# Row loads on ScalarE's queue, ranks in bf16 and norms behind the third round, in a fused Mamba, experts and attention kernel

## What is computed

```
Mamba:      norm, projection, convolution, a scan over 1024 positions with 16 states for each of
            256 channels, output projection, residual (the token stream is called X below)
experts:    p = softmax(norm(X) @ gate_W); the two best of 8 experts of each token;
            y = x + relu(x @ W1[e] + b1[e]) @ W2[e] + b2[e], mixed; norm, gain, add to X, norm
attention:  6 layers, 16 heads of 8, every token against all 1024 of its batch, softmax,
            a decay by distance, feed-forward 128-512-128, norms
last:       feed-forward with weights and activations rounded to 4-bit blocks of 16, residual
```

## Time and profile before

| | |
|---|---|
| median of 3 executions | 2826.67 us (2818.91 to 2829.14) |
| the profiled execution | 2813.64 us, its span 2811.8 us |
| busy in the span | DVE 2458.1 us (87%), PE 2392.2 (85%), ACT 2302.9 (82%), POOL 1433.5 (51%) |
| granted TensorE clock, mean | 0.94 of full speed |

### The profile page before, as it was taken

One profiled execution on the slowest core, in us unless ns is written; L12 is line 12 of the kernel. 1 busy time (PEld: TensorE's weight loads), 2 busy tenths in 40 slices (PEclk: granted clock), 3 DMA queues, 4 the chain that ended last, 5 costly groups with the idle time before them and its releaser, 6 DMA issues.

```text
span 2811.8 us, 93918 instructions
## 1 busy us (share of the span) xinstructions
PE 2392.2 (85%) x38335; PEld 1274.7 (45%) x38335; DVE 2458.1 (87%) x3438; ACT 2302.9 (82%) x4212; POOL 1433.5 (51%) x2865
## 2 busy tenths in 40 slices
PE   6778684788998998999889989899999998999856
PEld 3444473434444444444444444445444444444435
DVE  4988943699999999999999899999999999999956
ACT  5877632579998998999999899999999999999832
POOL 3443454235644665456644566445664456643564
PEclk8988887689999999999999999999999999999978
DMA  4000023413122131221222121221212212120000
GB/s 134 1 1 1 23 77 87 82 32 61 23 44 47 31 53 30 47 41 36 44 39 47 34 44 31 52 47 32 45 31 52 47 33 45 31 36 11 2 1 16
DMA packets 75119, 110.44 MB, mean 39 GB/s; under 512 B 7425, under 2 KB 69761, under 8 KB 72129
## 3 DMA queue, kind: packets, MB, share of 16 engines
q1 hardware_dynamic: 72256, 99.35, 18.5%
q0 software_dynamic: 2432, 5.08, 0.6%
HBM read 79.41 MB, written 29.05 MB: 39 GB/s over the span
## 4 chain that ended last, share of the span: by engine, by line
PE 38%; issue 18%; ACT 11%; DVE 11%; POOL 9%; DMA 1%; DVEq 0%; SPq 0%; ACTq 0%; POOLq 0%
PE bank L767 12%; PE bank L698 12%; PE bank L778 10%; ACT E L1038 9%; DVE NM L1409 7%; ACT acc L989 1%; POOL acc L1626 1%; POOL H L1636 1%; PE bank L679 1%; POOL H L1639 1%; POOL smp L1619 1%; DMA UNITB<-second 1%; PE bank L692 1%; POOL dg L1684 1%; ACT UB L1000 1%
## 5 line engine op out<-in xcount | busy, mean ns | idle before, releaser
L1409 DVE TENSOR_REDUCE NM<-bank 128x1 f32<-128x1024 f32 x1536 | 1800.2, 1208 | 82.4 <-PE bank L767 62.3
L1038 ACT ACTIVATE E<-bank,NM 128x1024 f32<-128x1024 f32 x1536 | 1707.5, 1118 | 189.0 <-DVE NM L1409 139.5
L767 PE MATMUL bank<-KS,QS 72*32 72x512 bf16 x12288 | 975.1, 390 | 163.5 <-ACT E L1038 113.7
L778 PE MATMUL bank<-E,dg 128*32 128x256 f32 x12288 | 941.2, 387 | 6.0 <-issue 4.2
L1684 POOL TENSOR_TENSOR dg<-mask,RZ 128x128 f32<-128x128 f32 x384 | 153.0, 398 | 863.7 <-DVE RZ L1419 758.4
L767 PEld LDWEIGHTS bank<-KS,QS 72*32 72x32 bf16 x12288 | 260.9, 96 | 706.3 <-ACT E L1038 583.2
L778 PEld LDWEIGHTS bank<-E,dg 128*32 128x32 f32 x12288 | 393.6, 112 | 297.0 <-issue 71.3
L1038 ACT ACTIVATION_READ_ACCUMULATOR E<-bank,NM 128x1 f32 x1536 | 310.6, 202 | 0.0
L1626 POOL TENSOR_TENSOR acc<-acc,rel 128x256 f32<-128x256 f32 x384 | 272.3, 729 | 7.8 <-ACT acc L989 7.8
L698 PE MATMUL bank<-H,ET 128*32 128x129 f32 x6144 | 194.9, 277 | 13.7 <-issue 7.3
L698 PEld LDWEIGHTS bank<-H,ET 128*32 128x32 f32 x6144 | 175.4, 111 | 41.5 <-issue 18.7
(11 more groups left out here) (262 smaller groups left out, 2651.7 us busy)
## 6 DMA issues: line engine op xcount, KB each, us to landing
KS<-scratch SPq DMA_DIRECT2D x72, 384.0 KB
QS<-scratch SPq DMA_DIRECT2D x216, 128.0 KB
scratch<-UB SPq DMA_DIRECT2D x144, 128.0 KB
WL<-in_wl SPq DMA_DIRECT2D x6, 1091.0 KB, 12.1
first<-in_fill SPq DMA_DIRECT2D x2, 990.0 KB, 8.2
second<-in_fill SPq DMA_DIRECT2D x2, 990.0 KB, 10.2
WAX<-first SPq DMA_DIRECT2D x2, 528.0 KB, 4.8
UNITB<-second SPq DMA_DIRECT2D x2, 528.0 KB, 13.5
```

The source lines that it names most:

```text
L767: inst = PE_.matmul(bank[x % 3][32 * i:32 * i + 32, k * 512:k * 512 + 512], QS[0:72, half % 2, 4 * hq + i, r0:r0 + 32], KS[0:72, b, 4 * hq ...
L778: inst = PE_.matmul(pb(6)[32 * k:32 * k + 32, 256 * grp:256 * grp + 256], dg[:, x // 4 % 3, x % 4, :], E[:, x % NE, :].rearrange("p (i k c ...
L1038: A_.activation(E[:, x % NE, :], bank[x % 3][:, :], ACT.Exp, bias=NM[:, x % 4:x % 4 + 1], accum_out=ZS[:, quad % 3, j:j + 1]).then_inc(s[" ...
L1409: V.tensor_reduce(NM[:, x % 4:x % 4 + 1], bank[x % 3][:, :], AX.X, ALU.max, negate=True).then_inc(s["rowmax"], 1)
```

## The change

1. `rows_of` for rounds 1 to 3 is issued by ScalarE's program, just before the round's first unit, and no longer by SP.
2. The registers are loaded at other places (`KNOWN`): for rounds 0 and 1 VectorE does it in steps 120 and 126 of the scan, TensorE at 122 and 149; for rounds 2 and 3 one to three steps ahead of the round. VectorE copies a unit's `W1` one step earlier.
3. `rank` works on bf16 copies (`OH`, `below`, `ones`) with 9 products for 16.
4. The second batch's gating (`G00` to `G30`) and its rank stand at 143 to 150, inside round 0 and ahead of round 1 (`ROUND[1]` 151), where most of it stood inside round 1. For this the last output product and its norm move ahead (`LASTLY`: `outp` at 137 for 144).
5. Three norms of the first batches and tiles (`n00`, `n01`, `n02`) go from VectorE to GpSimd, and `beta` is added earlier.
6. The first batch's `f0` to `n21` stand at 179 to 186, from the last units of round 2 on; the projections follow at 186 to 196, and round 3 starts at step 190 (184 before), after the first half's projection.
7. `KS` is laid out `[2, 2, 16, 512]` for `[2, 16, 1024]`, so that what `stack_k` writes to a partition is one run of 16 KB for 16 runs of 1 KB.

```diff
-DONE = {"PE": {16: "outp"}, "ACT": {}, "DVE": {4: "y2", 17: "x1"}, "POOL": {5: "yz0", 6: "yz1"}}
+DONE = {"PE": {14: "outp"}, "ACT": {}, "DVE": {4: "y2", 14: "x1"}, "POOL": {5: "yz0", 6: "yz1"}}
+LASTLY = {"PE": {9: "outp"}, "ACT": {}, "DVE": {4: "y2", 10: "x1"}, "POOL": {5: "yz0", 6: "yz1"}}
...
-ROUND = (133, 150, 167, 184)
+ROUND = (133, 151, 168, 190)
+KNOWN = {"PE": {122: 0, 149: 1, 167: 2, 189: 3}, "DVE": {120: 0, 126: 1, 166: 2, 187: 3}}
...
-        KS = sbuf(pk, "KS", [128, 2, NHEAD, L], BF16)
+        KS = sbuf(pk, "KS", [128, 2, 2, NHEAD, 512], BF16)
...
-        OH = sbuf(pm, "OH", [128, NT, 16])
+        OH = sbuf(pm, "OH", [128, NT, 16], BF16)
+        below, ones = sbuf(pm, "below", [128, 128], BF16), sbuf(pm, "ones", [128, 128], BF16)
...
                 for r, u in rounds(p):
-                    if u == 0:
-                        chosen = experts_of(e, mybir.EngineType.PE, r)
-                    unit_pe(e, r, u, chosen)
+                    unit_pe(e, r, u, chosen[r])
+                if p in KNOWN["PE"]:
+                    chosen[KNOWN["PE"][p]] = experts_of(e, mybir.EngineType.PE, KNOWN["PE"][p])
...
-                PE_.matmul(o[:, 0:128], mc_("below"), OH[:, batch(j), :].rearrange("p t c -> p (t c)"), start=True, stop=False)
+                PE_.matmul(o[:, 0:128], below[:, :], OH[:, batch(j), :].rearrange("p t c -> p (t c)"), start=True, stop=False)
+                PE_.matmul(o[:, 128:144], ones[:, :], OH[:, 8 * j + 7, :], start=False, stop=False)
                 for t in range(7):
-                    PE_.matmul(o[:, 16 * t + 16:128], mc_("ones"), OH[:, 8 * j + t, :].unsqueeze(1).to_broadcast([128, 7 - t, 16]), start=False, stop=(t == 6))
-                for t in range(8):
-                    inst = PE_.matmul(o[:, 128:144], mc_("ones"), OH[:, 8 * j + t, :], start=(t == 0), stop=(t == 7))
+                    inst = PE_.matmul(o[:, 16 * t + 16:144], ones[:, :], OH[:, 8 * j + t, :].unsqueeze(1).to_broadcast([128, 8 - t, 16]), start=False, stop=(t == 6))
...
@@ scan_act
                 for r, u in rounds(p):
+                    if r and u == 0:
+                        rows_of(e, r)
                     unit_act(e, r, u)
...
@@ scan_dve
+                for r, u in rounds(p + 1):
+                    if u < UNITS:
+                        weights_dve(e, UNITS * r + u, chosen[r][u])
...
@@ sync
             e.wait_ge(s["dtp"], 2 * CHUNKS)
-            rows_of(0)
+            rows_of(e, 0)
...
-            rows_of(1)
-            rows_of(2)
             mixed_of(0)
             store_qk(e, 0)
             stack_k(e, 0)
             stack_q(e, 0)
-            rows_of(3)
             store_qk(e, 1)
             stack_k(e, 1)
             mixed_of(1)
```

More of the change, by code:

```diff
@@ L66, in side @@
     for k in range(CHUNKS):
-        out += [(k, x) for x in DONE[engine].get(p - 32 * (k + 1), "").split()]
+        done = DONE if k < CHUNKS - 1 else LASTLY
+        out += [(k, x) for x in done[engine].get(p - 32 * (k + 1), "").split()]
         if k:
@@ L767, in scores @@
                         inst = PE_.matmul(bank[x % 3][32 * i:32 * i + 32, k * 512:k * 512 + 512], QS[0:72, half % 2, 4 * hq + i, r0:r0 + 32],
[L768 removed]
+                                          KS[0:72, b, k, 4 * hq + i, :], start=True, stop=True)
                 inst.then_inc(s["scores"], 1)
@@ L1176, in scan_dve @@
                 for r, u in rounds(p):
-                    if u == 0:
-                        chosen = experts_of(e, mybir.EngineType.DVE, r)
-                    unit_dve(e, own, r, u, chosen)
+                    unit_dve(e, own, r, u)
                 for j, x in gates("DVE3", p):
@@ L1193, in expert_dve @@
                 e.wait_ge(s["ld_moe"], 128)
+                own.count(V.tensor_copy(below[:, :], mc_("below")))
+                own.count(V.tensor_copy(ones[:, :], mc_("ones")))
                 for q in range(2):
@@ L1556, in expert_pool @@
                 G.tensor_tensor(EN[k][3][:, r], EN[k][2][:, r], mhalf[:, 0:4], ALU.pow).then_inc(s["epow"], 1)
+            elif p == "n0":
+                e.wait_ge(s["epow"], NORM[0, j] + 1)
+                for i in range(4 * j, 4 * j + 4):
+                    G.tensor_scalar(row(i), X[:, i, :], EN[0][1][:, i, 0:1], EN[0][3][:, i:i + 1], ALU.subtract, ALU.mult).then_inc(s["rn"], 1)
             elif p == "bet":
```

48 lines of the change are left out of this document (25 added, 23 removed), and 27 rows, old and new, of tables (GATES, PROJECT).

## The result

The changed kernel took 2790.11 us (median of 4 executions, 2785.40 to 2801.01) beside 2823.08 us for the kernel before (4, 2818.91 to 2829.14): ratio 0.9883, 95% interval 0.9861 to 0.9906, or 33 us less. The forecast was 2808 us, 18.4 us less. The direction and the place were right; the size was not, and the time lies at the lower end of the range. Three later comparisons of the same two kernels gave 0.9893 (0.9858 to 0.9928), 0.9880 (0.9841 to 0.9919) and 0.9929 (0.9910 to 0.9948).

The account below looks back on a forecast made before the run. It took attention to be bound by VectorE and ScalarE together, the seam by successive waits. Terms -2.6 - 2 - 6 - 2 - 5.8 = -18.4 us, from a median of 2826.67, gave 2808 us; range 2790 to 2821.

Parts of the forecast that it names:

- the scan: Up to round 0: norms and a register load leave VectorE, two register loads come in; -2.6 us (-8 to +3).
- round 0: Gating, last output product and a norm come earlier, filling GpSimd's idle time before the last scatter; -2 us (-2 to +2).
- round 1: The rank no longer stands between the units but mostly under the round trip before them; -6 us (-6.9 to -3).
- round 2 to the first keys: VectorE's 8.55 us wait at f0 goes, but units and norms overlap less; -2 us (-5 to +5).
- first keys to first scores: Earlier rows for round 3 shorten the key chain by 9.8 us, the layout costs 4; -5.8 us (+2 to -14).
- 27.3 + 5: At the seam: queries through 27.3 us after the first KS issue, then 5 us for the second half's six stores.
- From `KS` issued to the first scores is 14.6 us and stays.: At the seam's end: issue of KS to first scores unchanged at 14.6 us, but for the layout.
- +2 each: Each of two KS loads in the seam's chain slower by 2 us through the new layout.
- The rest: Attention and last feed-forward, behind the first scores: no change, since keys come 33.8 us or more ahead of use.
- A shorter seam: Rival, chance 0.20: layout no slower, stores in 3 us, register loads 1.2 each, perhaps 2 from norms; about 2797 us.
- The queue doesn't matter: Rival, chance 0.10: round 3's rows share DMA engines with KS and QS and arrive no earlier; 2815 us.
- Slower: Rival, chance 0.05: attention's key loads grow slow enough to delay the scores; 2844 us at 37 us a load.

Follow-up runs that it names:

- e13: The kernel before, unedited, profiled again on a chip without late signals; median 2814.77 us on that chip, first scores at 529.15 us.
- e14: The changed kernel, unedited, on the same chip as e13; ratio 0.9880 to the kernel before, first scores at 498.17 us.
- e7: The kernel before, unedited, profiled again on a chip with late signals; first scores at 546.55 us.
- e8: The changed kernel, unedited, on the same chip as e7; ratio 0.9893 to the kernel before, first scores at 512.25 us.
- e15: The kernel before with only the row loads of rounds 1 to 3 issued by ScalarE; 2793.74 us beside 2814.77, ratio 0.9930.
- e1: The kernel before with only the new KS layout; 2826.57 us beside 2829.69, ratio 1.0001.
- e2: The changed kernel with the old KS layout back; 2796.89 us, ratio 0.9898 to the kernel before.
- e9: The changed kernel with the second batch's gating, rank (still bf16) and last output product back at their old steps; ratio 0.9874 to the kernel before.
- e4: The changed kernel with the register loads of rounds 0 and 1 moved back next to the rounds; ratio 0.9891 to the kernel before.
- e16: The changed kernel with the second half's stores and keys ahead of the first half's queries on SyncE; 2777.43 us, ratio 0.9850 to the kernel before.
- e12: The changed kernel with the second half's six stores issued by ScalarE's queue at step 197; ratio 0.9896 to the kernel before.
- e18: The changed kernel, unedited, on a further chip with late signals; ratio 0.9929 to the kernel before, first scores at 515.01 us.
- e3: The changed kernel with SyncE issuing the rows of rounds 1 to 3 again; 2819.40 us, ratio 0.9961 to the kernel before.
- e5: The changed kernel with the first batch's f0 to n21 moved from steps 179 to 186 to 171 to 179; ratio 0.9903 to the kernel before.

## Why the prediction was right, and where it was wrong

The terms, by the pair from one chip of kind A (e13, e14), which is the kind the trace of before was taken on, and by the pair on B (e7, e8):

| term | forecast (bounds) | A | B |
|---|---|---|---|
| the scan (to round 0's start) | -2.6 (-8 to +3) | +0.4 | -3.6 |
| round 0 | -2 (-2 to +2) | -4.1 | -0.9 |
| round 1 | -6 (-6.9 to -3) | -8.8 | -14.4 |
| round 2 to the first keys | -2 (-5 to +5) | +1.2 | +11.0 |
| first keys to first scores | -5.8 (+2 to -14) | -19.8 | -26.5 |
| sum | -18.4 | -31.0 | -34.3 |

**The step that failed is the last term**, first keys to first scores: -5.8 us forecast, -19.8 measured on A. Its mechanism was right: the long wait of the earlier trace rows is gone, the queries' transfers run through round 3, and the first scores wait for `KS`, not for GpSimd. The second half's stores still land behind the queries, as I had said. Its size came out of three sub-steps, each wrong by 4 to 5.5 us.

- *From the first keys to the second half's.* I had 27.3 + 5; in e14 it is 26.8, 5.5 less. The 27.3 was the landing of round 3's first rows, which I took for the end of the queries. By the trace's packets the queries ended 26.0 us after the first keys were asked for in the trace of before, and 27.2 in e13, with the rows of round 3 moving beside them; in e15, without those rows, it is 22.4, in e14 23.3. That is 4.0 us. The stores need 3.5 more for my 5: half of their packets (384 of 768) have moved by 474.8, among the queries, and the other half starts at 482.5, just ahead of the queries' end at 484.2. That is 1.5 us.
- *"From `KS` issued to the first scores is 14.6 us and stays."* Those 14.6 us ended with GpSimd's last scatter and the fence; the load itself takes 10.5 in e14, 4.1 less. I read two rows and not what lies between them, though the chain of the trace of before shows the scatters there, the last of them ending at 530.31.
- *"+2 each" for the layout.* The key loads of e1, e2 and e15 show none of it, 4 less.

Together 13.6 us, which is the difference between -5.8 and -19.8 but for 0.4.

**Round 1** was right in kind: the 6.85 us of the rank go and nothing sticks out. On A it gave 2.8 us more than forecast. The load and the rank are done in 3.25 + 0.50 us (e14) where I had 3.1 to 7.4, but they lie ahead of the round's first transpose and don't shorten the round; and the gating pieces are not it either, since e9 has them inside the round at the same 26.0 us. e9 shows that bf16 would have sufficed without the move. In e13 the step that holds the rank takes 8.9 us for 1.23, 7.7 too many; what gave the rest stays open. On B the round lost 52.0 - 34.8 = 17.2 us more before and 11.6 more in the changed kernel: which goes with the chip and the place in the program, and which no row of the trace of before could show.

**The scan** came out at nothing on A instead of -2.6. The two register loads were dearer in my sum (4.8) than the trace has them (one gap of 1.31 us that e4 removes). What the sum had at nothing is the wait behind GpSimd's scatters, 4.57 us in e14: they stand in the upper bound ("if GpSimd's eight scatters of the first batch hold the sums up anyway"), but I had priced only GpSimd's own 1.8 us and not what stands ahead of it in its queue.

**Round 0** gave 4.1 us on A, outside my -2 to +2, but one pair can't carry that: three kernels on A that are alike up to there have 31.8, 33.7 and 36.0 us (e14, e16, e12). The start of round 0 scatters as well, 355.29 to 356.59 in the same three.

**Round 2** gave nothing on A, as its bounds allowed. On B it cost 11 us, because there, in the kernel before, the longer round 1 had given GpSimd time to finish: `H` is asked for 1.1 us after round 2's first transpose (9.6 in e13), and `f0` did not wait at all. The 2.5 us for the rising clock were worked out from no row; in e14 the clock stood at 0.50 until 4.4 us into the round.

**The rest** was left at nothing. My sign of being wrong, more than 5 us longer, shows in e14 (2288.4) and e18 (2287.6) against 2281.0, and not in the other two; since variants of the changed kernel have 2270 to 2282, I read it as drift, which is not shown. In e18 the changed kernel measured only 0.9929, though its first scores came as early as in the other profiles from B. The kernel before was not profiled on that chip, so whether its seam is shorter there or the rest of the changed one longer stays open.

**The signs.** No float32 rank, no wait at `f0`, the queries running through round 3 and first scores that wait for `KS` all came as said. Of the two gaps at the register loads one came (1.31 us, step 126). That the first profile of the change had its first scores at 514.52, inside my 510 to 515, was luck: on the kind of chip that I had reckoned from they come at 498.17.

**The rivals.** "A shorter seam" (2797) came nearest; of its reasons the layout and 1.5 of the 2 us on the stores held, and the one gap at a register load is 1.31 us for its 1.2. "The queue doesn't matter" is refuted by e3 and e15: part 1 alone has a ratio of 0.9930 where all parts have 0.9880. The rule of the Trainium skill, "DMA: Bandwidth & Descriptors", rules for kernel authors, that issuing from another engine gives no bandwidth, is not contradicted by this, and e12 agrees with it: its stores landed no sooner. What the rows gained was their place in an order: they no longer stood behind nine query loads, and did not move beside them. "Slower" by late keys did not happen.

## What to carry to other kernels

Before taking an interval between two rows as the price of a transfer, look at what ended it; here a scatter and a fence stood in for a load. Moving a round's loads to another engine's queue was worth about 0.7% here, alone (e15, 0.9930) and on top of the rest (e3 without it 0.9961, e8 with it 0.9893), and all other parts together about 0.4% (e3): what stood behind these loads in the program's order could start sooner. And take the profiles of both kernels from one chip before the difference is read term by term.

## What was not expected of the hardware

On two of four chips TensorE's signals arrived late, by 3.8 us in e7 and 7.6 us in e5, at two or three neighbouring units of round 1, nearly the same ones in each profile of a kernel, while GpSimd kept its pace of 1.27 us a scatter; the granted clock fell to 0.50 behind them. In round 1 this cost 17 us of 52 before and 12 of 38 after. On the other two chips no signal is late in that round in any kernel. The traces from B also hold fewer of the transposes' signals (45 to 56 for 60 transposes, 60 or 61 in the traces from A), so the size of a single delay is rough; the length of the round is not. What causes it the runs do not tell.
